# Dummy products on TensorE at the seams of three stages, and loads moved ahead, in a kernel of cross-attention and a feed-forward block with experts

## What is computed

```python
x = x + _L0_xattn_ref(_layernorm(x, axis=-1), ctx_1024, ctx_1024, mask, w_q, w_k, w_v, w_o)
x = x + _L0_ffn_ref(_layernorm(x, axis=-1), ...)

# _L0_xattn_ref: 16 heads of 16 columns, rotary positions on query and key
attn = jax.nn.softmax(where(mask == 0, -10000.0, query @ key_ / sqrt(16)), axis=-1)
x = (attn @ value) @ w_o.T

# _L0_ffn_ref: hidden_states (512 of its first axis hold the 4 items of the second)
qkv = _layernorm(hidden_states, ln1) @ qkv_weight.T     # 16 query heads, 4 key and value heads
hidden_after_attn = hidden_states + causal_attention(qkv) @ proj_weight.T
x = _layernorm(hidden_after_attn, ln2)
gate = jax.nn.softmax(x @ router_weight.T, axis=-1)
top_probs, top_idx = jax.lax.top_k(gate, 2)
expert_out[e] = _gelu(x @ w1[e]) @ w2[e]
return hidden_after_attn + sum over the two experts of top_probs * expert_out
```

## Time and profile before

| what | value |
|---|---|
| median of three runs | 857.69 us (856.13 to 857.75) |
| the profiled execution's own time | 855.98 us |
| its span in the trace | 854.2 us |
| mean granted TensorE clock | 0.892 of full speed |
| busy share PE / DVE / ACT / POOL | 81% / 66% / 58% / 43% |
| cross-attention, second block, experts | 548.1, 146.0 and 160.1 us |

### The profile page before, as it was taken

How to read it: one execution, slowest core, us unless ns; L and a number is a source line. 1 busy time by engine, 2 the same in 40 slices (tenths; PEclk the granted TensorE clock), 3 DMA queues, 4 the chain that set the end, 5 groups by cost and what they waited for, 6 DMA issues and landing times. The chain is left out here.

```text
span 854.2 us, 12963 instructions
## 1 busy us (share of the span) xinstructions
PE 695.6 (81%) x4120; PEld 412.9 (48%) x4120; DVE 566.6 (66%) x972; ACT 493.7 (58%) x954; POOL 363.1 (43%) x272
## 2 busy tenths in 40 slices
PE   4347899998999998999888988457876329999996
PEld 3233334443444434443333332356766318888885
DVE  5947767778777787778687842348687614555553
ACT  2011457778677775777666776265553226666663
POOL 4973606176034580043898920000143522445434
PEclk9675779999999999999899998568879558999999
DMA  9674453967458651238788820298312835523321
GB/s 266 210 206 139 167 171 96 292 192 231 141 167 237 211 160 72 77 97 228 233 281 269 281 116 1 68 362 332 44 66 63 277 93 134 108 33 38 37 31 19
DMA packets 60261, 133.31 MB, mean 156 GB/s; under 512 B 8996, under 2 KB 25940, under 8 KB 58740
## 3 DMA queue, kind: packets, MB, share of 16 engines
q1 hardware_dynamic: 33396, 73.51, 26.1%
q0 software_dynamic: 17360, 37.92, 17.1%
q10 hardware_dynamic: 9440, 21.06, 8.7%
HBM read 82.11 MB, written 70.70 MB: 179 GB/s over the span
## 5 line engine op out<-in xcount | busy, mean ns | idle before, releaser
L713 DVE TENSOR_REDUCE mx<-wide 128x2 f32<-128x1024 f32 x256 | 305.4, 1223 | 97.4 <-PE wide L836 96.9
L581 ACT ACTIVATE probs<-narrow 128x512 f32<-128x512 f32 x512 | 279.2, 598 | 102.4 <-PE narrow L863 100.6
L863 PE MATMUL narrow<-qst,kst 51*128 51x512 f32 x512 | 191.3, 468 | 12.5 <-ACT probs L581 6.4
L836 PE MATMUL wide<-kst,qst 49*128 49x512 f32 x512 | 159.7, 475 | 22.9 <-DVE mx L713 10.1
L863 PEld LDWEIGHTS narrow<-qst,kst 51*128 51x128 f32 x512 | 81.5, 191 | 170.0 <-ACT probs L581 114.6
L878 PE MATMUL values<-probs,vaug 128*17 128x512 f32 x1024 | 141.3, 625 | 0.7 <-ACT probs L581 0.7
L1557 POOL DMA_INDIRECT out<-res,token x39 | 60.9, 1560 | 99.4 <-DMA out<-res,token 62.0
L836 PEld LDWEIGHTS wide<-kst,qst 49*128 49x128 f32 x512 | 67.7, 197 | 45.6 <-DVE mx L713 29.0
L431 POOL TENSOR_TENSOR turn_b<-turn_a,tab 128x1024 f32<-128x1024 f32 x10 | 24.1, 2410 | 118.3 <-ACT turn_a L575 117.8
L1130 POOL DMA_DIRECT2D out<-h x4 | 5.3, 1337 | 129.5 <-DVE h L1313 129.5
L1582 ACT ACTIVATE h_hi<-narrow 128x512 fp32r<-128x512 f32 x39 | 23.3, 597 | 46.0 <-PE narrow L1659 46.0
(11 more groups left out here) (253 smaller groups left out, 1305.2 us busy)
## 6 DMA issues: line engine op xcount, KB each, us to landing
list_rows<-in_w ACTq DMA_DIRECT2D x56, 342.0 KB, 4.6
kst<-k_pieces SPq DMA_DIRECT2D x14, 784.0 KB
k_pieces<-turn_a SPq DMA_DIRECT2D x16, 512.0 KB, 4.8
w_hi<-w_hi SPq DMA_DIRECT2D x16, 512.0 KB
w_lo<-w_lo SPq DMA_DIRECT2D x16, 512.0 KB
qst<-q_pieces SPq DMA_DIRECT2D x14, 384.0 KB
turn_a<-in_w POOLq DMA_DIRECT2D x10, 512.0 KB, 5.7
w_hi<-turn_b POOLq DMA_DIRECT2D x10, 512.0 KB, 3.0
```

The source lines that it names most:

```text
L581: nc.scalar.activation(probs[:, n % NP, :], narrow[ring_no["score", n] % 3][:, :], ACT.Exp, scale=DK ** -0.5).then_inc(exp_done, 1)
L713: last = nc.vector.tensor_reduce(mx[quad % 2][:, qt, :, hp, kh], slot[:, :, :], axis=AX.X, op=ALU.max)
L836: last = nc.tensor.matmul(slot[:, i, :], qst[u % 3][r:r + R_MAX, h, P * qt:P * qt + P], kst[u % 3][r:r + R_MAX, h, 512 * kh:512 * kh + 512 ...
L863: nc.tensor.matmul(narrow[ring_no["score", n] % 3][:, :], kst[u % 3][r:r + R_ALL, h, P * kt:P * kt + P], qst[u % 3][r:r + R_ALL, h, :], st ...
```

## The change

It has five parts.

1. **Dummy products in cross-attention.** A new kind of job, "warm", multiplies the identity with itself (128x128, fp32) into a slot of the wide bank; nobody reads the result. The ten groups 118 to 127 get one between their second and third score. In `after` three stand ahead of `out`, three ahead of `oT` and eight ahead of `oP`.
2. **Dummy products in the second block and after.** `keep_clock` issues 22 ahead of `T(0,0)`, 10 ahead of `qkv(0,0)` and 8 ahead of `qkv(1,0)`, in the bank that the item writes next; the wait for the bank now comes ahead of them, the wait for data behind. After the last item PE waits for `place(3)` and issues 45, waits for `scattered[3]` and issues 12. The experts' block has 8 after `turn_y(0)`.
3. **Two banks for the first turns.** `T(0,1)` and `T(1,1)` go to the second bank. `T(0,1)` doesn't wait for `Thi(0,0)` any more, `T(1,k)` waits for `Thi(0,k)`, and `T2(0,0)` also for `Thi(1,1)`.
4. **Tables ahead.** After a `root` that an exponential follows, and after an `exps` or `rexp` that a square root follows, ACT runs an activation of one column, which makes its table load stand there. There are seven of these. One more, with gelu, stands at the head of the experts' block, ahead of `y_full` of the first tile.
5. **First two tiles early.** SP reads two starts in the second block, waits for all four `scattered`, and issues the fetch of tiles 0 and 1 into a buffer of their own, ahead of the end of the block. In the experts' block it begins with tile 2.

```diff
@@ attention_order
-        steps = [...] + [("job", j) for j in tops[:1]] + [("score", 4 * g + 2)]
+        steps = [...] + [("job", j) for j in tops[:1] or [("warm", g)] * (g > GROUPS - 11)] + [("score", 4 * g + 2)]
...
-    after = [("moments", 0), ("out", QUADS - 1), ("oT", B - 1), ("oP", B - 1, 0), ("oP", B - 1, 1)]
+    after = [("moments", 0), ("warm", GROUPS), ("out", QUADS - 1), ("warm", GROUPS + 1), ("oT", B - 1), ("warm", GROUPS + 2), ("oP", B - 1, 0), ("oP", B - 1, 1)]
...
+WARM = {GROUPS: 3, GROUPS + 1: 3, GROUPS + 2: 8}
...
+            elif kind == "warm":
+                for i in range(WARM.get(j[1], 1)):
+                    last = nc.tensor.matmul(slot[:, 0, 0:P], ident[:, :], ident[:, :], start=True, stop=True)
@@ second_block_order
-            add(("T", j, k), ("first", j), ("Thi", j, 0) if k else ("Thi", j - 1, KC - 1))
+            add(("T", j, k), ("first", j), ("Thi", j - 1, k) if j < 2 else ("Thi", j, 0) if k else ("Thi", j - 1, KC - 1))
@@ second_block, SP
+        sp.wait_ge(table_set, 2)
+        starts = [sp.value_load(table[0:1, 1, n:n + 1], min_val=0, max_val=ROWS - P) for n in range(EARLY)]
+        for j in range(QT):
+            sp.wait_ge(scattered[j], 16 * 8)
+        for n in range(EARLY):
+            sp.dma_start(y_first[:, n, :].bitcast(U32), list_dram[bass.ds(starts[n], P), :]).then_inc(y_in[n], 16)
@@ second_block, ACT
+        def load_table_for_next(item):
+            if tabled.index(item) + 1 < len(tabled):
+                comes = tabled[tabled.index(item) + 1][0]
+                if (comes == "root") != (item[0] == "root"):
+                    nc.scalar.activation(tiny[...], ident[:, 0:1], ACT.Sqrt if comes == "root" else ACT.Exp)
@@ second_block, PE
+        def keep_clock(bank, products):
+            for i in range(products):
+                nc.tensor.matmul(bank[:, 0:P], ident[:, :], ident[:, :], start=True, stop=True)
...
+                keep_clock(bank, WARM.get(item, 0))
+                pe.wait_ge(*by_act("first" if kind == "T" else "n2", j))
...
+        pe.wait_ge(*by_dve("place", QT - 1))
+        keep_clock(T_bank, WARM_END)
+        pe.wait_ge(scattered[QT - 1], 16 * 8)
+        keep_clock(T_bank, WARM_LANDED)
+
+EARLY = 2
+WARM_END, WARM_LANDED, WARM_FIRST = 45, 12, 8
+WARM = {("T", 0, 0): 22, ("qkv", 0, 0): 10, ("qkv", 1, 0): 8}
@@ experts_block
-        for n in range(TILES):
+        for n in range(EARLY, TILES):
...
+        nc.scalar.activation(tiny[:, :], ident[:, 0:1], ACT.Gelu_apprx_tanh)
         split_y(0)
...
         turn_y(0)
+        for i in range(WARM_FIRST):
+            nc.tensor.matmul(values[:, P:2 * P], ident[:, :], ident[:, :], start=True, stop=True)
```

More of the change, by code:

```diff
@@ L89, in steps_of @@
         tops = tops[len(early):]
-        steps = [("score", 4 * g)] + [("job", j) for j in early + first] + [("score", 4 * g + 1)] + [("job", j) for j in tops[:1]] + [("score", 4 * g + 2)]
+        steps = [("score", 4 * g)] + [("job", j) for j in early + first] + [("score", 4 * g + 1)] + [("job", j) for j in tops[:1] or [("warm", g)] * (g > GROUPS - 11)] + [("score", 4 * g + 2)]
         steps += [("weigh", g - 1)] * (g > 0) + [("score", 4 * g + 3)]
@@ L188, in on_pe @@
     def on_pe(j):
-        return j[0] in ("xT", "q", "k", "v", "max", "mxt", "out", "oT", "oP")
+        return j[0] in ("xT", "q", "k", "v", "max", "mxt", "out", "oT", "oP", "warm")
     def on_act(j):
@@ L995, in sem @@
         return ctx.enter_context(nc.semaphore(name))
-    router = sb("router", [P, KC, E_])
+    router, tiny = sb("router", [P, KC, E_]), sb("tiny2", [P, 3 * QT + 2])
     qkvw_hi = w2_hi[:, E_ - 1, :, :].rearrange("p f d -> p (f d)")[:, 0:KC * QKV].rearrange("p (k n) -> p k n", k=KC)
@@ L1082, in value, with first_bank @@
         return shared(j, s, D + EH * DK)
+    def first_bank(j, k):
+        return T2_bank if j < 2 and k == 1 else T_bank
     def turned_bank(j, k):
@@ L1140, in _ @@
     def _(act):
+        tabled = [item for item in order if item[0] in ("root", "exps", "rexp")]
+        def load_table_for_next(item):
+            if tabled.index(item) + 1 < len(tabled):
+                comes = tabled[tabled.index(item) + 1][0]
+                if (comes == "root") != (item[0] == "root"):
+                    nc.scalar.activation(tiny[:, tabled.index(item):tabled.index(item) + 1], ident[:, 0:1], ACT.Sqrt if comes == "root" else ACT.Exp)
         for item in order:
@@ L1499, with experts_block @@
 PIECES = 6
-def experts_block(nc, ctx, wide, narrow, values, w1, w2, ident, lncol, list_dram, out, table, keep, far):
+def experts_block(nc, ctx, wide, narrow, values, w1, w2, ident, lncol, list_dram, out, table, keep, far, y_first, y_in):
     (w1_hi, w1_lo), (w2_hi, w2_lo) = w1, w2
@@ L1522, in experts_block @@
     down_banks = [narrow[2][:, 0:D], values[:, 0:D]]
-    y_in = [sem(f"y_in{i}") for i in range(SLOTS)]
     y_turned, up_done, h_turned, down_done = sem("y_turned"), sem("up_done"), sem("h_turned"), sem("down_done")
@@ L1637, in turn_y @@
             for k in range(KC):
-                last = nc.tensor.transpose(y_banks[n % 2][:, k, :], y[:, n, P * k:P * k + P], ident[:, :])
+                last = nc.tensor.transpose(y_banks[n % 2][:, k, :], rows(n)[:, P * k:P * k + P], ident[:, :])
             last.then_inc(y_turned, 1)
@@ L1720, in program @@
         far = ctx.enter_context(nc.sbuf_tensor("far", [P, TILES], U32))
+        y_first = ctx.enter_context(nc.sbuf_tensor("y_first", [P, EARLY, WIDE], F32))
+        y_in = [ctx.enter_context(nc.semaphore(f"y_in{i}")) for i in range(SLOTS)]
         lncol = ctx.enter_context(nc.sbuf_tensor("lncol", [P, 4, KC], F32))
         with ExitStack() as part:
-            second_block(nc, part, io, xt, wide, narrow, values, w1, w2, split_dram, ident, lncol, mv1, list_dram, out, table, keep, far)
+            second_block(nc, part, io, xt, wide, narrow, values, w1, w2, split_dram, ident, lncol, mv1, list_dram, out, table, keep, far, y_first, y_in)
         with ExitStack() as part:
-            experts_block(nc, part, wide, narrow, values, w1, w2, ident, lncol, list_dram, out, table, keep, far)
+            experts_block(nc, part, wide, narrow, values, w1, w2, ident, lncol, list_dram, out, table, keep, far, y_first, y_in)
 def kernel(**inputs):
```

54 lines of the change are left out of this document (33 added, 21 removed).

## The result

The changed kernel took **847.43 us** in the median of four runs (847.40 to 849.31), the one before 857.72 (856.13 to 865.39) beside it: a ratio of 0.989, with a 95% interval from 0.985 to 0.9929. The forecast was 846, between 841.5 and 853. The ratios leave out executions over 1.5% above the fastest of their kernel, which the medians keep; without them the first of the two is 856.3 us against 857.1 before.

A forecast was written before the change was run, and what follows sets the result against it. Stretches at the seams, single chains from engine to engine run at about half clock, were taken as the part the change could shorten. Terms -6.3 - 0.5 - 5.0 = -11.8 us, from the median 857.69 to 846 us; range 841.5 to 853.

The forecast's parts named there:

- Part 1: Tail of cross-attention: dummies keep the clock full, so the last groups, turns and `oP` run warm; -6.3 us.
- I take it as kept: Tail of cross-attention: the claim that the clock stays full with the dummies, 7 in 10.
- Rival 1: Tail of cross-attention: the clock falls all the same, part 1 taken as 0, total -5.5, 852 us; chance 0.18.
- nothing: Tail of cross-attention: cost of the dummies if warm, as they fit into PE's waits, one per group into 0.45 us.
- my term for `oP`: End of cross-attention: 3.55 us of `oP` records would take 1.95 us at full clock, 1.6 us less.
- Part 2: Second block: early gain from clock and second bank, less the cost of moved table loads; -0.5 us, ends -4.5 and +2.7.
- The early gain: Start of the second block to the first score: -0.5 - 2.1 - 1.3 + 0.65 = -3.2 us.
- the others 0 to 0.2 each: Second block: moved table loads off the chain stand in ACT's idle time or beside work that doesn't end last.
- my other estimate: Second block: with a drain of about 1.38 us per table switch the block ends at +2.3, 849 us; chance 0.10.
- Part 3: Seam to the experts: later block end +1.35, early fetch -3.2, gelu load +0.6, clock -4.2, split wait +0.4; sum -5.0 us.
- the price of the dummies: Seam to the experts: a dummy takes 0.23 us warm and 0.43 cold, so the 45 take 12.7 us, the 12 take 2.8.
- rival 3: Mainly at the seam to the experts: dummies don't raise the clock and run cold, +12 us, 870; chance 0.05.

The follow-up runs named there:

- e2: Changed kernel with the tail's dummy table given its own name, so 3, 3 and 8 dummies run instead of 1, 1 and 1: 852.00 us.
- e12: e8 with wide dummies at the seam (11, and 1 behind the landing) and no dummy in the group that holds `out`: 848.05 us.
- e9: The kernel before, unchanged, in a second profile on chip C: one run, 851.46 us.
- e10: The changed kernel, unchanged, measured a third time, on chip C: 858.47 us.
- e4: Changed kernel without the 45, 12 and 8 dummies around the seam to the experts, early fetch kept: 851.76 us.
- e8: Changed kernel with only a gelu tiny activation, moved behind the last `rexp`; 3, 3 and 8 tail dummies; 4 instead of 12 behind the landing: 851.80 us.
- e11: Changed kernel with 11 and 3 products of 128x512 at the seam in place of 45 and 12 of 128x128: 852.75 us.

## Why the prediction was right, and where it wasn't

The number was right for the first measurement: -10.3 us against a forecast of -11.8, inside the range. Its parts were not all right, and on chips B and C the sum was not. That the first number came out so near is in part luck.

- **Part 1** (-6.3; profile -4.75). The step that failed lies ahead of "I take it as kept": not that the dummies hold the clock in the ten groups, where it held in eleven profiles of eleven, but that without them it is lost from 525.7 us to the end each time. The second profile of the kernel before took 42.12 us there, less than the changed kernel's 42.55. Rival 1 had the change worth nothing in the tail because the clock would fall all the same; it came near in size because it sometimes doesn't fall without. The sum of the terms was sound for a tail that runs cold: e2, with all dummies as written, took 41.48 us, 5.8 less than the first profile of before, and e12, without the one beside `out`, 6.7 less. Two terms were mis-stated: 3, 3 and 8 dummies cost nothing because they weren't there, and the one in the group with `out`, "nothing", cost 0.7 to 0.8. Where they are there, they give 1.1 to 1.5 us, close to my term for `oP` (1.6).
- **Part 2** (-0.5; +0.26). The early gain was 4.2 us (26.52 to 22.35) for my 3.2, though only 3.1 against e9 (25.48), and the load moved at the second tile's root cost 1.5 as forecast. The term "the others 0 to 0.2 each" with what follows was too small: in all the loads ahead cost 3.8 us over profiles, and I had 2.15. It isn't the drain by which my other estimate had the block at +2.3: no row has that drain.
- **Part 3** (-5.0; -5.10 in the first profile, but +2.5 on chip C, from 31.25 in e9 to 33.76 in e10). The step that failed is the price of the dummies, 0.23 us each from rows of other instructions: it held in the first measurement (12.9 and 2.9 us), but leaves out that TensorE can stand still for 6 us among 57 small ones, which it did on chips B and C. My slower case, rival 3, put the loss at this very place (PE the last to drain) by another cause, cold products. And the split of the -5.0 was wrong: in the pair that tells, the fetch gives 2.6 us (I had 3.2), dummies and what they do for the clock together 0.15, and the other 2.3 is a clock that rose sooner without any dummy.
- **The measurement.** 0.2% was too fine. With the spread named above, the four first runs (three within 0.04 us of each other) looked far surer than the kernel is. By the stretches (seam -4.4 to -5.1, second block 0 to +1, tail 0.4 of loss against e9 to a gain of 4.8 against the first profile) I estimate that the change is worth some 5 us where TensorE doesn't stand still at the seam. The ratio of e4 on chip A, whose stretches are those of the changed kernel within 0.2 us, bears this out: 0.9951 (0.9913 to 0.9989), some 4 us. Where it stands still, nothing can be measured. The profiled pair differs by 6.7 us, the first medians by 10.3; that the rest has to do with where cold stretches fell in the untouched part is likely, but no run shows it.

## What to carry to other kernels

A stretch at half clock in one profile may be a place where the clock can fall, not one where it must: look at a second profile of the same kernel before pricing its removal. Issue a fetch ahead of a barrier if its input is there: that was worth 2.6 us here, and the dummies around it 0.15. If TensorE is to be kept at work over a seam, use few, wide products instead of many small ones, and only in gaps that nothing else needs, since a barrier waits for dummies that run late. A table load moved ahead pays where ACT is idle at the new place (0.4 us for the gelu load in e8); behind a busy chain it delays the work that now stands behind it. And compare the counts of the instructions built with those written: 1, 1 and 1 stood where 3, 3 and 8 were meant.

## What the hardware showed that I had not expected

- TensorE stood still for 6.0 to 6.4 us in the middle of 57 small products (49 in e8) with nothing to wait for that the profile shows, in all five profiles of chips B and C that had those products there, and in none of the four others. Products of four times the width, a quarter as many, ran through on chip C (e11, e12).
- On the same two chips DVE's run of some 30 small instructions at this place took 7.0 to 12.1 us instead of 5.9, in the kernel before as well (6.97).
- The same code took cold stretches at different places of cross-attention from one profile to the next; from the first exponential to the last turn of maxima the fourteen profiles took between 412.9 and 425.7 us.
